# Graph layer on one core: TensorE in place of DMA transposes, and roots, results and screens in another order

## The reference

```
h = relu(layernorm(x))
q = round(min(h / alpha, 1) * 15)                  # 4-bit steps
w = quantised weight (3-bit steps)                 # 512 x 512
s = relu(q @ w * scale), rounded to steps 0..15    # the support
x = x + adj @ s * scale
h = relu(layernorm(x))
x = x + attention_factor @ h
```

## Time and profile before

| | |
|---|---|
| median of three runs | 148.74 us |
| profiled execution | 148.4 us, span 146.6 us |
| PE busy | 117.7 us (80%) |
| DVE busy | 114.5 us (78%) |
| ACT busy | 95.7 us (65%) |
| POOL busy | 74.3 us (51%) |
| DMA read / written | 24.66 MB / 6.30 MB |

### The profile page before, as it was taken

How to read it: one execution, slowest core, us unless ns; L and a number is a source line. 1 busy time by engine, 2 the same in 40 slices (tenths; PEclk the granted TensorE clock), 3 DMA queues, 4 the chain that set the end, 5 groups by cost and what they waited for, 6 DMA issues and landing times.

```text
span 146.6 us, 1939 instructions
## 1 busy us (share of the span) xinstructions
PE 117.7 (80%) x558; PEld 69.9 (48%) x558; DVE 114.5 (78%) x249; ACT 95.7 (65%) x145; POOL 74.3 (51%) x109
## 2 busy tenths in 40 slices
PE   0396999799978999699999999999996754998000
PEld 0392545455434563347475757575752623376000
DVE  0789999499799869959999997998329239999950
ACT  3678787758896897096919199999923941951100
POOL 2564423528527549700005798788788872621120
PEclk9999999999999999999999999999999997799965
DMA  5999999987996999998919558952435031050321
GB/s 147 338 412 422 387 411 362 253 186 167 315 297 195 221 272 334 402 395 266 393 10 297 209 192 248 336 183 79 125 107 179 18 107 72 0 217 0 143 107 47
DMA packets 18288, 32.44 MB, mean 221 GB/s; under 512 B 7841, under 2 KB 10658, under 8 KB 16738
## 3 DMA queue, kind: packets, MB, share of 16 engines
q1 hardware_dynamic: 15730, 24.29, 50.4%
q10 hardware_dynamic: 1584, 5.64, 13.1%
q0 software_dynamic: 960, 2.36, 5.5%
HBM read 24.66 MB, written 6.30 MB: 211 GB/s over the span
## 4 chain that ended last, share of the span: by engine, by line
DVE 29%; POOL 25%; issue 21%; DMA 6%; PE 5%; ACT 4%; DVEq 0%; POOLq 0%; ACTq 0%
POOL raw L820 10%; POOL narrow L832 9%; DMA h_iT<-h_i 6%; POOL rs L739 6%; DVE st L1012 5%; DVE sup L1057 4%; DVE most L1069 4%; PE acc L1358 3%; DVE ring L1119 3%; DVE sup_h L1056 2%; DVE x_sb L1257 2%; DVE lo L1063 1%; DVE h_qT L1052 1%; ACT h_i L555 1%; DVE mv L1017 1%
## 5 line engine op out<-in xcount | busy, mean ns | idle before, releaser
L1431 PE MATMUL acc<-sup,lo 128*128 128x512 f32 x128 | 31.9, 401 | 2.1 <-DVE lo L1112 2.1
L1425 PE MATMUL acc<-sup_h,hi 128*128 128x512 f16 x128 | 29.8, 387 | 0.0
L1431 PEld LDWEIGHTS acc<-sup,lo 128*128 128x128 f32 x128 | 23.9, 188 | 8.2 <-DVE lo L1112 2.6
L739 POOL TENSOR_TENSOR rs<-ve,minus_half 128x1 f32<-128x1 f32 (+2 forms) x21 | 19.8, 949 | 12.5 <-DVE ve L1022 12.2
L820 POOL DMA_INDIRECT raw<-adj_g,at_sb x12 | 14.5, 1211 | 19.6 <-DMA at_sb<-at_d 16.6
L536 ACT ACTIVATE junk<-raw,below 128x2048 uint8<-128x2048 f32 x12 | 23.9, 1990 | 0.1
L1376 PE MATMUL acc<-sup,lo 128*128 128x512 f32 x64 | 21.6, 449 | 0.5 <-DVE sup L1057 0.5
L585 ACT ACTIVATE ring<-x_sb,mv 128x512 f32<-128x512 f32 x15 | 10.2, 714 | 16.9 <-DVE ve L1022 11.7
L528 ACT ACTIVATE hi<-raw 128x2048 f16<-128x2048 f32 x7 | 13.3, 1904 | 11.7 <-PE acc L1431 7.6
L1119 DVE SCALAR_TENSOR_TENSOR ring<-ring,rs,x_sb 128x512 f32<-128x512 f32 x15 | 10.6, 749 | 12.2 <-POOL rs L739 6.9
L1425 PEld LDWEIGHTS acc<-sup_h,hi 128*128 128x128 f16 x128 | 12.1, 100 | 16.2 <-issue 3.4
(11 more groups left out here) (117 smaller groups left out, 150.2 us busy)
## 6 DMA issues: line engine op xcount, KB each, us to landing
raw<-adj_t SPq DMA_DIRECT2D x11, 1024.0 KB, 5.5
raw<-adj_t ACTq DMA_DIRECT2D x8, 512.0 KB, 5.2
out<-ring SPq DMA_DIRECT2D x15, 256.0 KB
x_sb<-x SPq DMA_DIRECT2D x3, 1024.0 KB, 14.2
sup_d<-sup_h SPq DMA_DIRECT2D x4, 512.0 KB
w_sb<-weight SPq DMA_DIRECT2D x4, 258.0 KB, 4.1
raw<-adj_t ACTq DMA_DIRECT2D x1, 1024.0 KB, 5.5
x_sb<-x SPq DMA_DIRECT2D x1, 512.0 KB, 5.9
```

The costliest lines, as they stand in the source:

```text
L739: nc.gpsimd.tensor_tensor(rs[:, a:a + m], ve[:, a:a + m], minus_half[:, 0:m], ALU.pow).then_inc(r_ready, 1)
L1425: nc.tensor.matmul(bank[:, cols], part(hi, k % PARTS, j), sup_h[:, j, cols], start=(j == 0), stop=False)
L1431: ins = nc.tensor.matmul(bank[:, cols], part(lo, k % PARTS, j), sup[:, j, cols], start=False, stop=(j == T - 1))
```

## The change

- `TURN`, `h_iT` and `h_turned` are gone. PE transposes every tile, between the halves of the products of tile j - 2, and `bound_hT` reads PSUM in all tiles. `round_h` waits for PE's transpose of the slot in all tiles.
- Chunk 4 of the adjacency is loaded from the ACT queue at j = 10.
- POOL takes roots in groups: tiles 0 to 3; 4 to 7 after the second six gathers; 8 after the third; 9 to 11 after the fourth; then singly. A root of several waits for the variance of the last of them.
- DVE makes residual 6 before results 0 to 3, residual 9 and the split of tile 12 before results 6 and 7, residuals 10 and 11 before result 8, and residual 13 before `split_rest(3)`.
- ACT makes `screen_ones` 4 to 9 earlier, three of them ahead of a `split_hi`, the high parts of tiles 12 and 14 before results' `relu2` of 6 and 9, and `screen_ones(11)` ahead of `split_high(3)`.

```diff
@@ sync
-            for j in range(TURN, T):
-                wait_h(sp, j)
-                if j >= TURN + 2:
-
-                    wait_hT(sp, j - 2)
-                sp.dma_start_transpose(h_iT[:, j % 2, :, :], h_i[:, j % SLOTS, :]).then_inc(h_turned[j % 2], 16)
-                if j == 11:
-
-                    load_adj(GT)
@@ round_h
-                if SLOTS <= j < SLOTS + TURN:
+                if j >= SLOTS:
                     act.wait_ge(hqT_in_psum, j - SLOTS + 1)
-                elif j >= SLOTS + TURN:
-                    act.wait_ge(h_turned[j % 2], 16 * ((j - SLOTS - TURN) // 2 + 1))
@@ scalar
-                if j == 8:
-
-                    act.dma_start(raw[:, 3, :], adj_t[3]).then_inc(adj_in[3], 16)
+                if j in (8, 10):
+
+                    k = 3 if j == 8 else GT
+                    act.dma_start(raw[:, k, :], adj_t[k]).then_inc(adj_in[k], 16)
             screen_ones(3)
+            screen_ones(4)
             split_hi(6)
-            screen_ones(4)
+            screen_ones(5)
+            screen_ones(6)
             split_hi(7)
-            screen_ones(5)
+            screen_ones(7)
+            screen_ones(8)
             split_hi(8)
-            screen_ones(6)
...
             split_hi(ordinal(10))
-            screen_ones(7)
+            screen_ones(9)
             relu2(4)
             relu2(5)
-            screen_ones(8)
             split_high(1)
             widen(1)
+            split_hi(ordinal(12))
             relu2(6)
             relu2(7)
-            split_hi(ordinal(12))
-            screen_ones(9)
             relu2(8)
+            split_hi(ordinal(14))
             relu2(9)
             split_high(2)
             widen(2)
-            split_hi(ordinal(14))
             screen_ones(10)
             relu2(10)
             relu2(11)
+            screen_ones(11)
             split_high(3)
             widen(3)
-            screen_ones(11)
@@ gpsimd
+        second_roots = [(0, GT), (4, 4), (8, 1), (9, 3)] + [(t, 1) for t in range(12, T)]
-            second_root(0, GT)
+            second_root(0)
             gather_rows(1)
             gather_sup(1)
-            second_root(4)
-            second_root(5)
+            second_root(1)
             gather_rows(2)
             gather_sup(2)
-            second_root(6)
-            second_root(7)
+            second_root(2)
             gather_rows(3)
             gather_sup(3)
-            for t in range(8, T - 1):
-                second_root(t)
+            for n in range(3, len(second_roots) - 1):
+                second_root(n)
@@ bound_hT
-                if j < TURN:
-                    dve.wait_ge(hqT_in_psum, j + 1)
-                    turned = psT_i[j % 2]
-                else:
-                    dve.wait_ge(h_turned[j % 2], 16 * ((j - TURN) // 2 + 1))
-                    turned = h_iT[:, j % 2, :, :].rearrange("p k i -> p (k i)")
+                dve.wait_ge(hqT_in_psum, j + 1)
@@ vector
             split_lo(8)
+            residual(6)
             for t in range(GT):
                 result(t)
-            residual(6)
             split_rest(0)
             residual(7)
...
             split_rest(1)
+            residual(9)
+            split_lo(ordinal(12))
             result(6)
             result(7)
-            residual(9)
-            split_lo(ordinal(12))
+            residual(10)
+            residual(11)
             result(8)
-            residual(10)
             split_rest(2)
-            residual(11)
             split_lo(ordinal(14))
             result(9)
             result(10)
             result(11)
             residual(12)
+            residual(13)
             split_rest(3)
-            residual(13)
             count_row()
@@ tensor
-                if j < TURN:
+                if j < T:
 
                     aggregate_first(j - 2, range(GT // 2))
                     transposes(j)
```

More of the change, by code:

```diff
@@ L55, in gnn_kernel @@
     EARLY = 2
-    TURN = 6
     AHEAD = 8
@@ L142, in gnn_kernel @@
         nb = sb("nb", [P, T], F32)
-        h_iT = over("h_iT", [P, 2, KD, P], I16, w_at)
         junk = over("junk", [P, CHUNK], U8, w_i_at)
@@ L237, in gnn_kernel @@
         hqT_in_psum = sem("hqT_in_psum")
-        h_turned = [sem(f"h_turned{b}") for b in range(2)]
         hqT_ready = sem("hqT_ready")
@@ L382, in second_no, with root_no @@
             return next(n + 1 for n, (a, m) in enumerate(second_ln) if a <= t < a + m)
+        def root_no(t):
+            return next(n + 1 for n, (a, m) in enumerate(second_roots) if a <= t < a + m)
         block = ctx.enter_context(nc.Block())
@@ L835, in gather_sup, with second_root @@
                     ).then_inc(sup_in[n], 16)
-            def second_root(t, m=1):
-                pool.wait_ge(var_ready, FIRST - EARLY + second_no(t))
+            def second_root(n):
+                t, m = second_roots[n]
+                pool.wait_ge(var_ready, FIRST - EARLY + second_no(t + m - 1))
                 inverse_root(t, m)
@@ L1041, in bound_hT @@
             def bound_hT(j):
-                if j < TURN:
-                    dve.wait_ge(hqT_in_psum, j + 1)
-                    turned = psT_i[j % 2]
-                else:
-                    dve.wait_ge(h_turned[j % 2], 16 * ((j - TURN) // 2 + 1))
-                    turned = h_iT[:, j % 2, :, :].rearrange("p k i -> p (k i)")
+                dve.wait_ge(hqT_in_psum, j + 1)
                 if j >= 2:
                     dve.wait_ge(sup_in_psum, j - 1)
-                nc.vector.tensor_scalar(h_qT[:, j % 2, :], turned, 0.0, ACT_LEVELS, ALU.max, ALU.min).then_inc(hqT_bounded, 1)
+                nc.vector.tensor_scalar(h_qT[:, j % 2, :], psT_i[j % 2], 0.0, ACT_LEVELS, ALU.max, ALU.min).then_inc(hqT_bounded, 1)
             def quantise_sup(i):
@@ L1117, in result @@
                 dve.wait_ge(yp_ready, t + 1)
-                dve.wait_ge(r_ready, FIRST + second_no(t))
+                dve.wait_ge(r_ready, FIRST + root_no(t))
                 nc.vector.scalar_tensor_tensor(ring[:, t % RING, :], ring[:, t % RING, :], rs[:, t:t + 1], x_sb[:, t, :],
@@ L1122, in last_result @@
             def last_result(t):
-                n = FIRST + len(second_ln)
+                n = FIRST + len(second_roots)
                 dve.wait_ge(out_stored[t % RING], 16 * (t // RING))
@@ L1384, in list_members @@
                 pe.wait_ge(value_ready, 1)
-                pe.wait_ge(hqT_bounded, TURN - 1)
+                pe.wait_ge(hqT_bounded, T - 1)
                 for e in range(2):
```

## The result

The changed kernel takes 140.87 us (median of four executions, 140.06 to 141.27), the kernel before beside it 149.51 us (148.14 to 152.29). The ratio is 0.944 with a 95% interval of 0.934 to 0.955: faster. The forecast was 142.7 us, with a range of 139.0 to 146.6.

The account below looks back on a forecast made before the run. Hand-overs between engines, not one full engine, were taken to bound the kernel. Span 146.6 + 0.4 front - 6.4 rear = 140.6, plus 1.8 and 0.3 for execution and median, gave 142.7 us; range 139.0 to 146.6.

Parts of the forecast that it names:

- Rear: Rear stage: reordered roots, results and residuals remove PE waits of 2.13 and 3.67 us, result 12 at 127.7; -6.4 us.
- Front: Front stage to 62 us: ten TensorE-transposed steps, 29.0 plus 0.9 and 0.2, against 29.71 us; +0.4 us.
- The sum: Whole kernel: span 146.6 + 0.4 - 6.4 = 140.6, plus 1.8 for execution and 0.3 for the median; 142.7 us.
- part 1: Front stage: TensorE instead of DMA transposes tiles 6 to 15, +0.4 us; moved loads and removed waits costed at nothing.
- Part 2: Rear stage, ACT: one more screen before each of three high splits; costed at nothing, covered by PE's dense tiles.
- The rule against the row: Rear: skill's rule says DVE splits don't delay POOL gathers; a profile row shows 0.96 stretched to 3.05 us; row followed.
- Rival C: Rear: no lock on gathers or no wait for root 9; result 12 at 124.0, -10.1, 139.0 us; chance 0.12.
- A: Front: DVE holds up half of the ten steps at 3.76 us; +3.6 instead of +0.4, 145.9 us; chance 0.13.
- B: Rear: POOL stays the bound through locks and a slow merged root, last root near 124, 146.3 us; chance 0.12.
- D: Front: transpose, bound and support become serial on every tile, ten steps of 4.0 us, +10.3, 152.6 us; chance 0.04.
- E: Rear: stalls only move, a merged root waiting for a residual that itself waits; change worth nothing, 148 us; chance 0.06.

Follow-up runs that it names:

- e7: Changed kernel with residuals 12 and 13 ahead of results 9 to 11 on DVE; 138.02 us, ratio 0.925.
- e1: Kernel before with only the TensorE transposes of tiles 6 to 15 and chunk 4 loaded from ACT; 148.39 us, ratio 0.982.
- e10: Kernel before, unedited, with another profiled execution; 152.22 us in the median.
- e2: Kernel before, DMA transposes kept, with the changed kernel's rear orders on ACT, POOL and DVE; 144.69 us, ratio 0.945.
- e11: Changed kernel with the ten DMA transposes issued as well, into a tile nobody reads; 140.62 us, ratio 0.939.
- e3: Changed kernel with ACT's rear order as before; 142.08 us, ratio 0.938.
- e6: Changed kernel with each DVE split of a dense tile made in four instructions; 138.82 us, ratio 0.931.
- e12: Changed kernel, unedited, run and profiled again; 140.93 us, ratio 0.939.
- e4: Changed kernel with POOL's roots 4 to 14 single and where they stood before; 144.21 us, ratio 0.955.
- e5: Changed kernel with DVE's rear order as before, POOL's merged roots and ACT's order kept; 141.88 us, ratio 0.948.

## Why the prediction was right, step by step

**Rear, -6.4 us forecast, -7.3 measured** (result 12 at 126.75 against 134.08). The mechanism is the one forecast. POOL's run of gathers and roots ends at nearly the same time in both kernels (119.83, when result 8 starts in the one before, and 119.47); what the new order does is to let DVE do some 7 us of work ahead of that time. Behind it DVE has 14.25 us to result 12 in the kernel before (119.83 to 134.08) and 7.17 in the changed one (119.58 to 126.75). DVE has no idle time from 119.83 to its end in the kernel before, so PE's wait of 3.67 us there, and the granted clock of 0.50 behind it (123 to 125 us), cost nothing by themselves. The layout on DVE's queue held nearly row by row: split of tile 10 forecast at 96.2 and found at 95.93, merged root ready at 100.1 and 100.11, split of tile 12 at 105.9 and 105.80, root of 8 at 109.7 and 109.84, split of 14 at 114.4 and 114.19. The last root was ready at 119.5; I had worked out 119.9 and taken 120.4. These 0.9 us are the difference between -6.4 and -7.3. That the wait for the root of 9 to 11 is late next was right (3.10 us; I gave 3.7), and e7, whose rear is 3.1 us shorter, shows what it was worth.

**Front, +0.4 us forecast; +0.2 in the profiled pair (57.2 to 57.4), and -3.0 in the medians of e1 and its neighbour.** That the pair agrees is luck, for the size of this term failed in two ways. First, tile 11's step was to be 3.76 us and tile 12's 0.2 longer than 2.90; they were 3.97 and 3.91. DVE's timeline there, the reduction, the bound and the two writes of tile 10's support:

```profile
42.40 1.22 DVE L1054 TENSOR_REDUCE most<-raw 128x8 f32<-128x1024 f32 x1
43.53 0.42 DVE L1037 TENSOR_SCALAR h_qT<-acc 128x512 bf16<-128x512 int16 x1
43.86 1.22 DVE L1041 TENSOR_SCALAR sup_h<-z_sup 128x512 f16<-128x512 int16 x1
45.00 1.37 DVE L1042 TENSOR_SCALAR sup<-z_sup 128x512 fp32r<-128x512 int16 x1
```

The writes take 1.22 and 1.37 us, though 0.28 and 0.42 elsewhere, because POOL's first two low pieces (43.78 to 46.10) run beside them; I had named this effect only for the end of the front. From tile 5 to tile 15 the ten steps take 31.6 us, 1.9 more than before, and not 30.1. These 1.9 us vanish behind the support of tile 15, in a stretch for which the sum had no term: the kernel before takes 6.76 us from there to tile 4's products (55.28 to 62.04) and waits 0.25 and 1.08 us for `sup` and `sup_h`; the changed kernel takes 5.04 (56.87 to 61.91) without these waits. Second, my sum compared with one execution of the kernel before. e10 and e2 show fronts 6.0 and 5.6 us longer by late landings and the slower clock behind them, e1 shows 3.0 us less in the median than its neighbour. The waits for the DMA were in the profile, their variation was not, except as a spread of 2 us in three times; I had no row for it and should have kept it as an open end toward a gain.

**The sum.** Of the 1.8 us between 142.7 and 140.87, 0.9 are the root and 0.2 the front; the rest is that the median lies 0.4 us below the profiled execution, where I had put it 0.3 above.

**The rest of part 1** cost nothing, as said: chunk 4 came in time, the bound from PSUM took 422 ns in the mean of the 15 that the trace holds, and e11 leaves no traffic effect.

**Part 2 at nothing:** e3, 0.1 us in the rear.

**The rule against the row.** The row was right for the sum, and I had drawn too much from the rule. In the changed kernel a gather that starts under a split of 2.28 us takes 1.90 to 2.71 us and ends 0.81 to 0.84 us after the split; between quarters of 0.6 us it takes 1.32 to 1.44 (e6), and beside none 0.95. But a gather that starts first is not held: that of 95.35 takes its 0.95 us though the split starts at 95.93, and in e12 one that starts 0.08 us ahead of a split (82.87 and 82.95) takes 0.94. So only a step at the start of a gather waits, not the rest of the issue. The Trainium skill (SBUF — State Buffer, Who interferes with whom) infers that such a subtraction does not hold up the writing of descriptors, and the gathers that start first agree with it. The same section says that a DVE instruction with two SBUF inputs does contend with a GpSimd instruction that reads SBUF, and each gather reads its row numbers from `at_sb` in SBUF. That this read is what waits fits the rows; it isn't shown by itself. The prediction's step from the rule to gathers that are not delayed left this read out. Rival C had the wait for the root of 9 to 11 gone, and it stands at 3.10 us.

**Rivals A, B, D, E.** A and D asked for many long steps: there are two. B asked for a last root near 124; it was ready at 119.47. For A the prediction says that tiles 2 to 5 run at 2.90 us; the trace has two such steps there, 2.91 and 2.90, and one of 1.33. E asked for stalls that only move; DVE's waits for roots and relus shrank from 12.2 to 5.1 us in sum.

## What to carry to other kernels

Look for the small instruction that a queue holds back: a 0.6 us root behind six gathers kept 5 us of DVE idle and 3.7 us of PE, and e4 and e5 show that moving the root is worth more (6.3 us) than reordering the waiting engine (4.4 us), each with ACT's new order, which e3 puts at 0.1 in the rear. Ask which of the two idle times is paid for: here it was DVE's, since DVE never rested again. When an engine waits for such a result, put independent work that is already possible ahead of the waiting instruction (e7), and cut a long instruction that locks another engine out into pieces (e6), but expect only one of the two gains where both fill the same wait. A term of a prediction that contains a DMA on the path should be taken from more than one execution: one profile had the front at 57 us, the next at 63. And a wait of PE can cost more than its length, when the granted clock falls behind it: 1.9 us more in e10.

## What was not expected of the hardware

A DMA transpose of one 128x512 int16 tile within the core's memory took 2.4 to 7.4 us from issue to landing in two executions of one kernel, and up to 7.9 in e2; four PE transposes of the same tile took 0.40 us in each of tiles 2 to 15. Two `tensor_scalar` writes of DVE (128x512 from int16) went from 0.28 and 0.42 us to 1.22 and 1.37 beside POOL's subtraction of 1.2 us, so each of the two engines can hold up the other. And in e12 the same program had a rear 1.0 us shorter than in the other profile, with a wait before results 4 and 5 of 1.00 us and not 2.00: POOL's first gather started 0.4 us earlier (77.55 against 77.94), and other gathers met the splits.
